# Quantisation parameters in group 0, the context quantised one step ahead, and another order behind the last step

## The reference

```python
x = x + attn(_layernorm(x))      # a state-space block: 128 heads of 64 in 8 groups
x = x + xattn(_layernorm(x), ctx_4096)
x = x + ffn(_layernorm(x))       # permute, 16 heads 32 -> 128 -> 32 with gelu, permute back

def xattn(x1, x2):               # both operands quantised to 8 bits, then one product
    fake_quant = lambda x, s, z: (clip(round(x / s + z), 0, 255) - z) * s
    return fake_quant(x1, s1, z1) @ fake_quant(x2, s2, z2)
```

## Time and profile before

| | us |
|---|---|
| median of 3 runs | 818.63 |
| range of the runs | 818.46 to 819.87 |
| span of the profiled execution | 819.7 |
| TensorE busy | 792.3 (97%) |
| VectorE busy | 714.0 (87%) |
| GpSimd busy | 588.2 (72%) |
| ScalarE busy | 543.9 (66%) |

### The profile page before, as it was taken

How to read it: one execution, slowest core, us unless ns; L and a number is a source line. 1 busy time by engine, 2 the same in 40 slices (tenths; PEclk the granted TensorE clock), 3 DMA queues, 4 the chain that set the end, 5 groups by cost and what they waited for, 6 DMA issues and landing times.

```text
span 819.7 us, 14437 instructions
## 1 busy us (share of the span) xinstructions
PE 792.3 (97%) x4242; PEld 618.8 (75%) x4244; DVE 714.0 (87%) x928; ACT 543.9 (66%) x1129; POOL 588.2 (72%) x484
## 2 busy tenths in 40 slices
PE   7988999999999999999999999999999999997988
PEld 5866878777887778877778877787877777775554
DVE  6999989898899989998899989898989989798653
ACT  3686677676677766776676775767767667885242
POOL 6287877887778877788778779787779758884100
PEclk9989999999999999999999999999999999999899
DMA  7362444433443344443444443344443445520001
GB/s 232 115 239 88 154 155 168 159 112 129 166 166 141 107 154 148 166 154 122 146 146 148 154 160 128 123 151 154 166 166 114 142 167 153 188 75 11 1 1 52
DMA packets 44050, 111.13 MB, mean 136 GB/s; under 512 B 5748, under 2 KB 6644, under 8 KB 44020
## 3 DMA queue, kind: packets, MB, share of 16 engines
q1 hardware_dynamic: 44020, 110.76, 39.7%
HBM read 109.30 MB, written 1.44 MB: 135 GB/s over the span
## 4 chain that ended last, share of the span: by engine, by line
PE 87%; DVE 8%; issue 2%; ACT 2%; SPq 1%; DMA 0%; DVEq 0%; ACTq 0%
PE ps_in L1279 16%; PE ps_in L1281 15%; PE ps_in L1280 15%; PE ps_y L1392 8%; PE ps_o L1279 7%; PE ps_o L1281 7%; PE ps_o L1280 7%; PE ps_y L1395 3%; PE ps_t L1354 3%; DVE hid L982 1%; DVE e L1038 1%; PE ps_o L1573 1%; PE ps_t L1366 1%; PE ps_t L1404 1%; PE ps_o L1557 1%
## 5 line engine op out<-in xcount | busy, mean ns | idle before, releaser
L530 POOL TENSOR_TENSOR w_lo<-raw,w_hi 128x512 fp32r<-128x512 f32 x144 | 233.4, 1642 | 110.4 <-ACT w_hi L639 109.0
L1279 PE MATMUL ps_in<-h_hi,w_hi 128*128 128x512 f32 x560 | 227.5, 406 | 0.0
L1281 PE MATMUL ps_in<-h_hi,w_lo 128*128 128x512 f32 x560 | 220.1, 393 | 0.0
L1280 PE MATMUL ps_in<-h_lo,w_hi 128*128 128x512 f32 x560 | 218.8, 391 | 0.0
L694 ACT ACTIVATE e<-e,nag 128x256 f32<-128x256 f32 (+1 forms) x512 | 183.6, 444 | 0.6 <-POOL e L550 0.6
L982 DVE SCALAR_TENSOR_TENSOR hid<-ps_in,curc,hid 128x510 f32<-128x510 f32 x186 | 138.3, 744 | 4.4
L1279 PEld LDWEIGHTS ps_in<-h_hi,w_hi 128*128 128x128 f32 x560 | 105.9, 189 | 31.0 <-issue 10.9
L659 ACT ACTIVATE hid<-ps_in,curc 128x512 f32<-128x512 f32 x62 | 48.2, 778 | 115.1 <-PE ps_in L1281 114.8
L1281 PEld LDWEIGHTS ps_in<-h_hi,w_lo 128*128 128x128 f32 x560 | 105.7, 189 | 23.6
L1280 PEld LDWEIGHTS ps_in<-h_lo,w_hi 128*128 128x128 f32 x560 | 106.2, 190 | 20.6
L561 POOL TENSOR_TENSOR e<-e,gm 128x512 f32<-128x512 f32 x64 | 100.4, 1568 | 27.3 <-DVE gm L1026 27.1
(11 more groups left out here) (237 smaller groups left out, 1237.0 us busy)
## 6 DMA issues: line engine op xcount, KB each, us to landing
e<-acs_rows SPq DMA_DIRECT2D x64, 768.0 KB, 4.4
raw<-in_w_in SPq DMA_DIRECT2D x144, 256.0 KB, 4.7
rawo<-in_w_out SPq DMA_DIRECT2D x64, 256.0 KB, 4.0
craw<-in_ctx SPq DMA_DIRECT2D x8, 256.0 KB, 2.8
res<-in_x SPq DMA_DIRECT2D x4, 256.0 KB, 3.3
out_x<-res SPq DMA_DIRECT2D x4, 256.0 KB, 2.2
acs_rows<-z SPq DMA_DIRECT2D x3, 128.0 KB, 2.0
rawo<-in_w_dt SPq DMA_DIRECT2D x1, 256.0 KB, 4.3
```

The lines of the kernel that those rows point to most:

```text
L530: pool.tensor_tensor(w_lo[:, slot, :], raw[:, slot, :], w_hi[:, slot, :].bitcast(F32), ALU.subtract).then_inc(s_lo, 1)
L1279: pe.matmul(dst, lh, rh, start=first, stop=False)
L1280: pe.matmul(dst, lh, rl, start=False, stop=False)
L1281: return pe.matmul(dst, ll, rh, start=False, stop=last)
```

## The change

1. `craw` has four slots instead of two, with a semaphore each. Loads 0 and 1 are issued before step (7,0), load t + 2 in step t, and load c waits for tile c - 4 to be kept.
2. Scaling and rounding of context tile t stand in step t (before: of tile t - 1), keeping of tile t - 1 in step t (before: t - 2). Of the context, only one keeping is left behind the last step.
3. `quant_params` is cut in three. `quant_steps` (the bf16 identity, reciprocals and small sums) stands at the end of step (0,6), `quant_terms` (a row and two products) at the end of step (0,7), `perm_numbers` (the two casts) at the end of step (7,0).
4. Behind the last step the queues have another order. VectorE: `decays_diagonal` of the last tile ahead of `skip_and_gate` of the one before, `gated` of the last tile ahead of `z_low` of the one before, all `one_hot` behind the last `z_low`. ScalarE: the gate tanh of tile 6 ahead of the last `exps`, that of tile 7 ahead of the last `cast_out`, the cast of the later weights `up` last. GpSimd: both `decays_off` first, then sums and splits alternately, `up_lo` behind `group_rms`.
5. `s_oin` now counts three of the four parts of the last output tile, and VectorE waits for each part in its turn.

```diff
@@ -34,6 +34,7 @@
+C_RING = 4
...
-        craw = sb("craw", [P, 2, D])
+        craw = sb("craw", [P, C_RING, D])
...
@@ -432,9 +433,9 @@
             def load_context(c):
-                wait(sp, s_q2, c - 1)
-                sp.dma_start(craw[:, c % 2, :], ctx_in[c // DK, (c % DK) * P:(c % DK + 1) * P, :])\
-                  .then_inc(s_ctx[c % 2], 16)
+                wait(sp, s_q2, c - C_RING + 1)
+                sp.dma_start(craw[:, c % C_RING, :], ctx_in[c // DK, (c % DK) * P:(c % DK + 1) * P, :])\
+                  .then_inc(s_ctx[c % C_RING], 16)
 
...
@@ -451,8 +452,8 @@
                 load_out(*lagged(n, t, 1))
-                if is_last(n):
-                    load_context(t)
+                if is_last(n) and t + 2 < CT:
+                    load_context(t + 2)
 
...
@@ -480,6 +481,8 @@
             sp.dma_start(perm_col_i[:, :], perm_by_part).then_inc(s_perm, 16)
+            load_context(0)
+            load_context(1)
             for t in range(CT):
...
@@ -617,14 +620,14 @@
             decays_off(last_m, CT - 2)
+            decays_off(last_m, CT - 1)
             add_square(last_m, CT - 3)
             split_out(last_m, CT - 2)
-            decays_off(last_m, CT - 1)
+            add_square(last_m, CT - 2)
             split_out(last_m, CT - 1)
-            add_square(last_m, CT - 2)
+            group_rms(last_m)
             pool.wait_ge(s_uph, 1)
             pool.tensor_tensor(up_lo, up_raw, up_hi.bitcast(F32), ALU.subtract).then_inc(s_upl, 1)
-            group_rms(last_m)
 
...
@@ -709,14 +712,14 @@
 
-                act.wait_ge(s_ctx[c % 2], 16 * (c // 2 + 1))
+                act.wait_ge(s_ctx[c % C_RING], 16 * (c // C_RING + 1))
                 act.wait_ge(s_qd, 1)
-                act.activation(craw[:, c % 2, :], craw[:, c % 2, :], ACT.Relu, scale=qd[:, 1:2], bias=qs[:, 3:4])\
+                act.activation(craw[:, c % C_RING, :], craw[:, c % C_RING, :], ACT.Relu, scale=qd[:, 1:2], bias=qs[:, 3:4])\
                    .then_inc(s_cs, 1)
 
             def context_keep(c):
                 act.wait_ge(s_cc, c + 1)
-                act.activation(q2[:, c, :], craw[:, c % 2, :], ACT.Identity, bias=offset[:, :]).then_inc(s_q2, 1)
+                act.activation(q2[:, c, :], craw[:, c % C_RING, :], ACT.Identity, bias=offset[:, :]).then_inc(s_q2, 1)
 
...
@@ -740,10 +743,10 @@
                 cast_out(*lagged(n, t, 2))
-                if is_last(n) and t >= 2:
-                    context_keep(t - 2)
                 if is_last(n) and t >= 1:
-                    context_scale(t - 1)
+                    context_keep(t - 1)
+                if is_last(n):
+                    context_scale(t)
                 tap0(n, ("h", t))
...
@@ -802,19 +805,17 @@
             last_m = GROUPS - 1
+            gate_tanh(last_m, CT - 2)
             exps(last_m, CT - 1)
-            gate_tanh(last_m, CT - 2)
-            context_scale(CT - 1)
-            context_keep(CT - 2)
+            context_keep(CT - 1)
             cast_out(last_m, CT - 2)
             z_high_and_square(last_m, CT - 2)
+            gate_tanh(last_m, CT - 1)
             cast_out(last_m, CT - 1)
-            context_keep(CT - 1)
-            gate_tanh(last_m, CT - 1)
+            z_high_and_square(last_m, CT - 1)
             act.wait_ge(s_ffw, 32)
             act.wait_ge(s_in, NIN * GROUPS)
             act.activation(up_hi, up_raw, ACT.Copy).then_inc(s_uph, 1)
-            z_high_and_square(last_m, CT - 1)
             act.preload_act_table(ACT.Gelu)
...
@@ -938,18 +939,24 @@
 
-            def quant_params():
-
-                dve.wait_ge(s_pp, 4)
-                dve.tensor_copy(ident_b[:, :], ident[:, :])
+            def perm_numbers():
+
                 dve.wait_ge(s_perm, 32)
                 dve.tensor_copy(perm_row[:, :], perm_row_i).then_inc(s_pk, 1)
                 dve.tensor_copy(perm_col[:, :], perm_col_i[:, :]).then_inc(s_pk, 1)
+
+            def quant_steps():
+
+                dve.wait_ge(s_pp, 4)
+                dve.tensor_copy(ident_b[:, :], ident[:, :])
                 for k in range(2):
                     dve.reciprocal(qd[:, k:k + 1], qs[:, 2 * k:2 * k + 1])
                     dve.tensor_scalar(qd[:, 2 + k:3 + k], qs[:, 2 * k + 1:2 * k + 2], -128.0, None, ALU.add)
                 step_of(dve.tensor_tensor(qd[:, 4:5], qs[:, 0:1], qs[:, 2:3], ALU.mult))
                 step_of(dve.tensor_scalar(qd[:, 5:6], qd[:, 2:3], -1.0, None, ALU.mult))
+
+            def quant_terms():
+
                 dve.wait_ge(s_iota, 1)
...
@@ -1115,8 +1122,14 @@
                     mean_square(n - 1)
-                if is_last(n) and t >= 1:
-                    context_round(t - 1)
+                if is_first(n) and t == CT - 2:
+                    quant_steps()
+                if is_first(n) and t == CT - 1:
+                    quant_terms()
+                if is_last(n) and t == 0:
+                    perm_numbers()
+                if is_last(n):
+                    context_round(t)
 
...
@@ -1157,7 +1170,6 @@
                     step(n, t)
-            quant_params()
             for t in range(CT):
...
@@ -1165,15 +1177,13 @@
             turned(last_m, CT - 1)
+            decays_diagonal(last_m, CT - 1)
             skip_and_gate(last_m, CT - 2)
-            decays_diagonal(last_m, CT - 1)
+            gated(last_m, CT - 1)
             z_low(last_m, CT - 2)
-            context_round(CT - 1)
-            gated(last_m, CT - 1)
-            one_hot(0)
             skip_and_gate(last_m, CT - 1)
             z_low(last_m, CT - 1)
-            for k in range(1, DK):
+            for k in range(DK):
                 one_hot(k)
...
@@ -1211,9 +1221,12 @@
             dve.wait_ge(s_r, GROUPS)
-            for pair, ready in (((0, 1), (s_oin, 1)), ((2, 3), (s_ou, STEPS))):
-                dve.wait_ge(*ready)
+            for pair in ((0, 1), (2, 3)):
                 for t in pair:
+                    if t < TT - 1:
+                        dve.wait_ge(s_oin, t + 1)
+                    else:
+                        dve.wait_ge(s_ou, STEPS)
                     add_output(t)
...
@@ -1430,7 +1443,7 @@
                                   (wo_hi[:, q % WO_RING, :], wo_lo[:, q % WO_RING, :]), q == 0, q == CT - 1)
-                    if is_last(m) and q == CT - 1 and t == 1:
+                    if is_last(m) and q == CT - 1 and t < TT - 1:
                         last.then_inc(s_oin, 1)
```

More of the change, by code:

```diff
@@ L240, in decoder_layer @@
         s_rows = [sem(f"rows_loaded{i}") for i in range(E_RING)]
-        s_ctx = [sem(f"context_loaded{i}") for i in range(2)]
+        s_ctx = [sem(f"context_loaded{i}") for i in range(C_RING)]
         s_hi = sem("w_hi_done")
@@ L356, in decoder_layer @@
         up_hi, up_lo = (w[:, DK, :].rearrange("p (k m) -> p k m", k=DK) for w in (w_hi, w_lo))
-        colrow = craw[0:1, :, :]
+        colrow = craw[0:1, 0:BATCH, :]
         f_hi, f_lo = h_hi, h_lo
@@ L961, in context_round @@
                 dve.wait_ge(s_cs, c + 1)
-                dve.tensor_scalar(craw[:, c % 2, :], craw[:, c % 2, :], 255.0, MAGIC, ALU.min, ALU.add)\
+                dve.tensor_scalar(craw[:, c % C_RING, :], craw[:, c % C_RING, :], 255.0, MAGIC, ALU.min, ALU.add)\
                    .then_inc(s_cc, 1)
```

## The result

| | before | after |
|---|---|---|
| median of the runs, us | 818.63 | 810.53 |
| range of the runs, us | 816.62 to 820.45 | 809.67 to 814.53 |
| span of the profiled execution, us | 819.7 | 808.7 |

The ratio of the runs is 0.9898, with a 95% interval from 0.9872 to 0.9925: 6.1 to 10.5 us faster. The forecast was 810.2. The changed kernel measured a second time, beside other runs of the kernel before, had 0.9930 (0.9908 to 0.9952), 3.9 to 7.5 us. So the gain is some 6 to 8 us, and a sum of stretches is needed to see whether the steps of the forecast were right or only its total.

What follows compares the result with a forecast made beforehand. TensorE, 87% of the span, was taken as the bound, so only its waits and lower clock count. 3.87 - 0.9 + 5.4 = 8.4 us off the 818.63 median gave 810.2, range 807.0 to 813.6.

Steps and rivals of the forecast that it cites:

- The head of the last group: Step (7,0): taking quant_params away shortens it from 14.16 to 10.29 us, a gain of 3.87 us.
- Group 0: Steps (0,6) and (0,7): the moved quant_steps and quant_terms delay the decay product; cost 0.9 us, ends 0 and 4.0.
- two-block case: Group 0: GpSimd blocks two quant_steps operations, delaying the decay product by 3.3 us, 1.45 too late; time 810.8.
- The end of (7,0): Two casts and one more rounding, about 1.0 us, covered by VectorE's 1.19 us idle; cost taken as nought.
- The bound given beside it: End of (7,0): without the idle cover, the step loses at most two more lock waits, 2.6 us.
- The drain: Behind the last step: TensorE's waits shrink, VectorE's eight one_hots set the first add_output; gain 5.4 us, ends 2.6 and 7.1.
- the first wait: Drain: TensorE's 1.19 us stall goes, as the rounding ahead of the first decay product shrinks from 1.52 to 0.42 us.
- All of it: Rival, chance 0.13: group 0 hides its part and TensorE sets the drain; gain 11.0 us, time 807.6.
- GpSimd wins the turns: Rival, chance 0.14: GpSimd's drain sum of squares starts before the second decay product; one lost turn 811.5, two 812.8.
- Group 0 stalls: Rival, chance 0.10: two blocks in each of two steps, a wait over 2 us and lower clock; cost 4.0, time 813.3.
- It does not do what it says: Rival, chance 0.05: the stall at the last group's start stays, only the drain gains; 813.2, or less gain with group 0.
- Slower: Rival, chance 0.03: TensorE's clock drops through the 128 products of lines 1544 to 1573, costing 18.7 us; 829.

Runs made afterwards that it cites:

- e3: Kernel before with only the context's slots, loads, scaling and rounding one step ahead; 816.04 against 819.58 us, ratio 0.9954.
- e8: Kernel before with only the changed order behind the last step and the finer s_oin waits; 814.56 against 819.58 us, ratio 0.9928.
- e2: Changed kernel with all three pieces of quant_params back between steps (6,7) and (7,0); 813.18 against 819.58 us, ratio 0.9924.
- e4: Changed kernel with quant_steps at the end of step (0,5) instead of (0,6); 812.24 against 818.01 us, ratio 0.9913.
- e9: Changed kernel without quant_steps: identity cast, reciprocals and sums in the prologue, product and negation heading quant_terms; 811.23 against 819.50 us, ratio 0.9911.
- e1: Kernel before with only quant_params cut in three and placed as in the change; 819.01 against 819.58 us, ratio 0.9987.
- e5: Changed kernel with the two permutation casts at the end of step (7,4) instead of (7,0); 811.06 against 818.01 us, ratio 0.9908.
- e10: e9 with the two casts and four one_hots between last z_low and mean square, the other four one_hots later; 809.63 against 819.50 us, ratio 0.9891.
- e6: Changed kernel with the mean square ahead of the last pair of one_hots; 812.98 against 818.01 us, ratio 0.9926.
- e7: Changed kernel with quant_steps in (0,5), casts in (7,4) and mean square ahead of the last one_hot pair; 810.02 against 818.01 us, ratio 0.9891.
- a_again: Changed kernel, unchanged, measured a second time beside other runs of the kernel before; 813.36 against 819.50 us, ratio 0.9930.

## Why the forecast came out right, step by step

**The head of the last group: right.** 3.87 forecast, 3.89 measured. By e3 and e8, 2.2 us of it are the wait that follows quant_params in all four traces that have it there (before, e2, e3, e8); the 1.6 of lower clock came in before and e2, not in e3 and e8. The forecast took a clock seen in one execution as a sure gain; that before's trace held it and gave the 3.89 was luck.

**Group 0: the mechanism right, the size half.** I took 0.9 between one block and two, all of it in (0,7); the loss was 1.90. (0,7) itself lost 0.75. Two operations were blocked there, but each met a split that was already running, so they took 1.96 us longer than free ones (1.32 and 1.01, in before 0.22 and 0.15), and not twice 1.28. They are the two that I named by the rule of the Trainium skill (SBUF — State Buffer, "Who interferes with whom"), and the trace agrees: 1.32 us for the cast and 1.01 for the product of two SBUF columns. The tensor-scalar forms that the rule lists as well were not blocked on one column (0.13 us for each of the two sums beside the split), and nothing was lost on the reciprocals. That the rule's two-block case, 1.45, is nearer to 1.90 than my value is chance, since it was reckoned for (0,7) alone. The step that failed is (1,1), which both had at nothing: 1.15 of the 1.90 appear there, two steps later. VectorE lost a further turn to GpSimd there (the decay product took 2.31 us for 1.21) and TensorE waited 0.82 for z, at a clock of 1.00. e4 and e9 show that it goes with quant_steps; I reckoned TensorE's delay in the same step and stopped there. quant_terms cost nothing that I can see: its first operation took 0.27 us unblocked at 109.74, as reckoned.

**The end of (7,0): wrong, within its bound.** I wrote that an idle 1.19 us covers 1.0 us of casts and rounding, and took nought; it cost 0.99 in (7,1). The failed step is the size of the small cast, "under 0.2": blocked by GpSimd it took 1.26, and the decay product behind the rounding, now overlapping the next GpSimd operation, 2.32. e1 shows that the casts alone are covered (11.66), e5 and e10 that the rounding alone nearly is (11.74), and e5 that the pair costs as much or more in another step (1.44). The bound given beside it, two more lock waits, held.

**The drain: right in its end and for the reason given, wrong in the first wait, and 0.7 more behind it.** Set on the forecast's scale (the drain began 3.39 us later in before: 739.01 against 735.62), the second decay product starts at 741.78 where I had 741.25, the first one_hot at 751.07 for 751.3, the last tile ends at 756.29 for 755.95, and the first add_output is at 755.53 for 755.85. The gain to there is 5.69 for 5.4. VectorE with its eight one_hots sets that end, as forecast; e6 and e10 show it. Two details failed. The first wait kept 0.73 of its 1.19, where I had it gone. What I gave for it, GpSimd waiting for the exponentials, did come (the rounding took 0.42 us), but VectorE reached the first decay product 0.67 us later against TensorE's turn than in e2. Of this 0.38 is the z product in front, at 732.56, which met decays_off and took 1.27 us (0.89 in e2). Another 0.32 was there before: in (7,7) VectorE scaled the turned tile 0.96 us after the start of the turn, in e2 0.64, with 0.31 of idle time ahead of it. The traces with the new order fall into two kinds. Where TensorE stood still for 1.4 us or more within the last group (e2 and e8 at its head, e5 and e7 in (7,5)), the z product took 0.89 to 0.99 and the first wait was at most 0.19; in a_again, e4, e6, e9 and e10, as in after, 1.27 to 1.29 and 0.73 to 0.77. The two go together in all ten, and I read it so: a VectorE that is given no such pause comes to the drain late, and 0.66 of what the move of the parameters gains at the head of the group is lost again here. And I held the 1.7 us that TensorE is ahead to end wholly in a later wait: 0.73 came out before the quantised product.

**The sum.** By steps: 3.87 - 0.9 + 5.4 = 8.4 forecast; 3.89 - 1.90 - 0.99 + 6.42 = 7.4 measured, with 5.69 and 0.73 for the drain and behind it. Two costs too small by 2.0 us stood against a gain too small by 1.0. The runs are at 8.1 and 6.1, so that the forecast's total is so near to the first of them is in part luck.

**The rivals.** *All of it* fell: group 0 paid and VectorE set the end. *GpSimd wins the turns* fell: its sum of squares began at 738.49, 0.10 us behind the second decay product, and was itself the one to wait (2.28 us, while the product took 1.23). *Group 0 stalls* fell in size: no wait there over 0.82. *It does not do what it says* fell for the head; e1 shows how near the parameters alone come to no gain. *Slower*, by the clock of the closing stage: a_again did run it at 0.84, and lost 2.74 us to after, a small part of the 18.7 priced. Before's own 20.36 is between them, and the other kernels of this study had 18.96 to 21.79, with no order by their edits, so I take it for chance and not for an effect of the change; why it varies stays open.

## What to carry to other kernels

When small operations are moved beside another engine's long ones, cost each at its blocked length, and follow the lateness two steps on, not only to the first wait. A step that is idle for 1.2 us covers one blocked operation and not two; better is a place where the other engine is still, as the prologue and the end of (0,7) were for the small operations here (the second still cost 0.17 us, since the decay product behind them met the split). And a pause taken away from one place can come back in another: an engine that caught up in it arrives late at the next. Before crediting a lower clock behind a wait, see whether it follows that wait in more than one execution.

## What was unexpected of the hardware

- The 46 steps from (1,2) to (6,7) took 517.73 to 517.75 us or 518.65 to 518.66, nothing between, over 13 traces. The changed kernel itself had one value in after and the other in a_again. It is 0.17% of equal work, and its cause is open.
- The same wait of 2.2 us on TensorE was followed by a granted clock of 0.88 over the step (before, e2) or of 1.00 (e3, e8): 14.1 us or 12.5.
- The closing products took 18.96 to 18.98 us, 20.36 to 20.53, or 21.76 to 21.79 with the same instructions, at a clock of 1.00 at one end and 0.84 at the other.
- A one-column product of VectorE, 0.15 us beside an idle GpSimd, took 1.01 beside a running one (e9, after).
- A lead of 0.06 to 0.08 us over GpSimd's splits was enough for VectorE at the head of (1,1): its decay product then took 1.21 us, and 2.30 to 2.31 where the splits started 0.51 to 0.52 ahead of it.
